# New stage order in the two query stages, the doubled columns copied by ScalarE, and the weight loader moved between the pieces of the lifting

## Chip, cores and metric

One Trainium2 chip, one core. The metric is the device time of one execution in microseconds (us); lower is better. Five engines work in the kernel: TensorE (PE), VectorE (DVE), ScalarE (ACT), GpSimd (POOL) and SyncE (SP, which here only issues DMAs). Each engine takes its instructions in order; between engines they are ordered by semaphores that are written by hand.

## The reference

Two transformer layers run one after the other on x of 8 samples x 512 tokens x 320 features, with a context of 8 x 64 x 192. Layer 0 is plain; layer 1 rounds q, k, v and the softmax weights to 8 bits with one step for the whole tensor.

```python
# layer 0
h1 = _ln(x, n1_g, n1_b)
x = _attn(h1, h1, q1, k1, v1, o1_w, o1_b, heads) + x
h2 = _ln(x, n2_g, n2_b)
x = _attn(h2, context, q2, k2, v2, o2_w, o2_b, heads) + x
h3 = _ln(x, n3_g, n3_b)
...
# layer 1: the same shape, with
q = fq_sym(x @ Wq)            # k, v alike; 20 heads of 16
scores = jnp.einsum('bhnd,bhmd->bhnm', q, k) * dh ** (-0.5)
w = fq_zero(jax.nn.softmax(scores, axis=-1))
out = jnp.einsum('bhnm,bhmd->bhnd', w, v)
```

fq_sym needs the largest magnitude over the whole tensor before any element can be rounded. So in layer 1 the projections are stored first and rounded in a later stage.

## The kernel before

The residual stream x stays in SBUF (x_resid). The program is a row of stages, each a block that every engine enters and leaves together: first loads, context projections, a dense stage with q, k and v (layer 0), self attention, a dense stage with q (the query of the cross attention), cross attention, the feed-forward stage; then the same for layer 1. The change touches three stages: the two dense stages with q ("the query stages", one per layer), and the first block of layer 1's self attention (exact_self_attention).

**A query stage** (dense_phase with main == "q", L497). A sample is 512 tokens in four tiles of 128. Its steps are: oT 0 to 2 (the attention output is turned on PE, in layer 0 only, and split by ACT and DVE into oT_hi and oT_lo; in layer 1 it comes by feature and is only split), oproj 0 to 3 (eight matmuls each, then DVE adds the bank to x_resid, L943), stats (DVE bn_stats, bn_aggr, var_eps, then POOL's power for rstd, L749), norm (DVE writes the normalized rows z, 320 columns and then 64 doubled ones in columns 320 to 383, for each of the four tiles, L959 and L962), zT 0 to 2 (PE turns z, L793; ACT writes h and hT_hi, DVE the difference hT_lo, L969), and q 0 to 2 (eight matmuls each into one of two banks outp; ACT copies the bank to st_hi, L911; then DVE makes st_lo in layer 0, L991, or the maximum in layer 1, L995). The doubled columns exist since the third tile of features has only 64, and the products take its high and low part as two halves of the partitions.

The order of the steps is one list, body, that all engines walk (loop, L624). The table ahead says for which sample a step is done in round i: q for sample i, stats, norm and zT for i + 1, oproj for i + 2 as oT 2, and oT 0 and 1 for i + 3. Every group of banks (oT, oproj, zT, outp) has two banks. On SP a sample's attention output is loaded as soon as that of the one before has been read, and q is stored as it comes out. In layer 0 POOL also splits the weights of the feed-forward stage between the samples (PoolLoader, L226). In layer 1 it adds the next bias to x_resid behind z_ready (L758).

**The first block of layer 1's self attention** (exact_self_attention, L1314). Each sample has a piece of q and of k (128 x 1280) and two of v; POOL loads, scales, rounds and splits them (L1572 to L1598), SP stores the results and loads them back as the stacks q_stack and k_stack, of which there are two. PE makes the 80 score tiles of a sample (L1497), DVE takes the maximum of each (L1531), ACT the exponentials and their sum (L1551). The stack of sample b is loaded when PE is through with sample b - 2. After its last piece POOL loads and splits the weights for what follows (26 jobs of 128 columns: Wq2, Wo1, Wff1) and adds the bias to the eight samples of x_resid (EarlyBias, L290):

```python
                    early.load(pool)
                    for i in range(len(loader.jobs) + 1):
                        loader.turn(pool, i)
                    for b in range(BATCH):
                        early.add(pool, b * TT, TT)
```

The second block of that stage (L1609 on: shifts, transposed scores, exponentials, output products) needs all five engines to have left the first.

## Time and profile before

| | us |
|---|---|
| median of 3 runs (3498.48 to 3504.57) | 3503.2 |
| the profiled execution | 3501.81 |
| its span in the profile | 3500.1 |
| PE busy | 2954.8 (84%) |
| DVE busy | 2168.7 (62%) |
| ACT busy | 1887.1 (54%) |
| POOL busy | 792.6 (23%) |

The page of the profile gives busy time over the whole span. The program is a row of stages with different limits, so the shares alone don't tell what a change in one stage is worth. The trace can be asked for the busy time in a stretch, for the instructions of one engine in order of time (with the idle time ahead of each and who ended it), and for the sum of waits by line. A duration in the timeline can reach a little into the next instruction's, since the engines overlap the end of one with the start of the next. Where instructions follow each other without idle time, the distance of their starts is what each costs.

### The profile page before, as it was taken

Reading aid. Unit: us, or ns where it says so; the run is one execution under the profiler, and the core shown is the slowest. Engines: PE = TensorE matmul, PEld = TensorE weight load, DVE = VectorE, ACT = ScalarE, POOL = GpSimd, SP = SyncE. Lnnn points to the kernel's source line nnn. Section 1 sums busy time; section 2 is a strip of 40 time slices with the busy share of each in tenths; the row PEclk is TensorE's granted clock in tenths of the full one; section 3 lists DMA queues with packets and bytes.
Section 4 is the critical chain, followed back from the end, with each engine's and each line's share of the span. In section 5 each row is a group of like instructions: output and inputs, shape, how many; then the busy total and the mean of one; then the engine's idle time right before and its main releaser. Section 6 shows DMA issues by size and latency. Waiting matters only on the chain. (4 is left out here: it accounts for less than half of the span.)

```text
span 3500.1 us, 47844 instructions
## 1 busy us (share of the span) xinstructions
PE 2954.8 (84%) x15582; PEld 1792.7 (51%) x15594; DVE 2168.7 (62%) x3896; ACT 1887.1 (54%) x3197; POOL 792.6 (23%) x1128
## 2 busy tenths in 40 slices
PE   5979999967697999998959999349987577699999
PEld 3754444456454888886821111011116442588888
DVE  4668888746353443445659999348876586344443
ACT  3427888833253232323559999459983356232322
POOL 0022122113651000000035545820001173200000
PEclk8979999988698999998965555555558899899999
DMA  6653333234662000002586465317532221200000
GB/s 188 209 172 99 104 106 105 83 96 115 147 179 55 10 10 18 9 0 71 151 184 154 105 144 94 62 37 100 83 60 68 74 70 64 57 25 26 16 24 15
DMA packets 369947, 296.61 MB, mean 85 GB/s; under 512 B 186343, under 2 KB 294431, under 8 KB 369759
## 3 DMA queue, kind: packets, MB, share of 16 engines
q1 hardware_dynamic: 361518, 277.73, 32.8%
q0 software_dynamic: 6128, 14.59, 1.7%
q10 hardware_dynamic: 2112, 1.97, 0.3%
q8 instruction: 96, 1.57, 0.2%
q14 instruction: 93, 0.75, 0.1%
HBM read 177.54 MB, written 114.52 MB: 83 GB/s over the span
## 5 line engine op out<-in xcount | busy, mean ns | idle before, releaser
L1297 DVE TENSOR_REDUCE neg_max<-nat 128x1 f32<-128x512 f32 x640 | 400.7, 681 | 66.3 <-PE nat L1160 66.0
L1497 PE MATMUL nat<-k_stack,q_stack 48*128 48x512 bf16 x640 | 380.7, 604 | 70.8 <-DMA k_stack<-k1w 30.2
L1531 DVE TENSOR_REDUCE m_all<-nat 128x1 f32<-128x512 f32 x640 | 423.3, 690 | 17.9 <-PE nat L1497 17.6
L1551 ACT ACTIVATE nat<-nat,m_all 128x512 f32<-128x512 f32 x640 | 427.7, 2128 | 2.9 <-DVE m_all L1531 2.8
L749 POOL TENSOR_TENSOR rstd<-var_eps,neghalf 128x4 f32<-128x4 f32 x48 | 49.0, 1020 | 1592.0 <-DVE var_eps L955 1591.9
L1551 ACT ACTIVATION_READ_ACCUMULATOR nat<-nat,m_all 128x1 f32 x640 | 403.7, 1673 | 0.0
L975 DVE SCALAR_TENSOR_TENSOR ff<-outp,bias,gel 128x512 f32<-128x512 f32 x160 | 120.1, 750 | 419.3 <-PE outp L377 419.3
L1233 ACT ACTIVATE probs<-sT 128x1024 f32<-128x1024 f32 x320 | 328.0, 1027 | 92.4 <-PE sT L1169 84.1
L895 ACT ACTIVATE gel<-outp,bias 128x512 f32<-128x512 f32 x160 | 110.0, 688 | 351.0 <-PE outp L377 351.0
L1730 ACT ACTIVATE exps<-sT 128x1024 f32<-128x1024 f32 x320 | 293.4, 1573 | 7.1 <-PE sT L1679 7.1
L899 ACT CAST ff_hi<-ff 128x512 fp32r<-128x512 f32 x160 | 99.1, 620 | 312.0 <-DVE ff L975 312.0
L1497 PEld LDWEIGHTS nat<-k_stack,q_stack 48*128 48x128 bf16 x640 | 63.8, 101 | 387.3 <-ACT nat L1551 351.1
L1767 DVE TENSOR_SCALAR probs<-exps 128x1024 bf16<-128x1024 f32 x320 | 218.1, 692 | 64.5 <-ACT exps L1730 64.5
L1160 PE MATMUL nat<-k_stack,q_stack 48*128 48x512 f32 x640 | 200.2, 523 | 26.1 <-DMA k_stack<-k_hi 17.3
L1679 PE MATMUL sT<-q_stack,k_stack 51*128 51x512 bf16 x640 | 194.2, 604 | 31.2 <-DMA q_stack<-shift 8.8
L1187 PE MATMUL o_ps<-probs,v_stack 128*32 128x256 f32 x2560 | 199.2, 393 | 1.1 <-issue 1.1
L978 DVE TENSOR_TENSOR ff_lo<-ff,ff_hi 128x512 fp32r<-128x512 f32 x160 | 120.2, 751 | 109.7 <-ACT ff_hi L899 109.7
L969 DVE TENSOR_TENSOR hT_lo<-h,hT_hi 128x512 fp32r<-128x512 f32 x144 | 105.7, 734 | 124.2 <-ACT hT_hi L890 124.1
L1160 PEld LDWEIGHTS nat<-k_stack,q_stack 48*128 48x128 f32 x640 | 79.8, 192 | 169.3 <-DVE neg_max L1297 132.1
L1169 PE MATMUL sT<-q_stack,k_stack 51*128 51x512 f32 x640 | 157.2, 429 | 0.5 <-ACT probs L1233 0.2
L793 PE MATMUL zT<-ident,z 128*128 128x128 f32 x384 | 68.0, 309 | 75.4 <-DVE z L962 64.6
L377 PE MATMUL outp<-hT_hi,Wff_hi 128*128 128x512 f32 x320 | 125.9, 393 | 3.9 <-DVE hT_lo L969 3.9
(495 smaller groups left out, 7180.2 us busy)
## 6 DMA issues: line engine op xcount, KB each, us to landing
v<-vpad SPq DMA_DIRECT2D x64, 320.0 KB, 2.8
q_stack<-q_part SPq DMA_DIRECT2D x90, 160.0 KB, 6.0
k_stack<-k1w SPq DMA_DIRECT2D x90, 160.0 KB, 11.1
q_stack<-q_hi SPq DMA_DIRECT2D x160, 64.0 KB, 2.6
k_stack<-k_hi SPq DMA_DIRECT2D x160, 64.0 KB, 2.2
v_stack<-v SPq DMA_DIRECT2D x40, 256.0 KB, 3.1
q_stack<-q_hi SPq DMA_DIRECT2D x80, 128.0 KB, 2.7
raw<-v SPq DMA_DIRECT2D x16, 640.0 KB, 15.1
```

Of the source, the lines that this page charges most:

```text
L377: mm = pe.matmul(out, stay, move, start=(n == 0), stop=(n == len(terms) - 1))
L1160: pe.matmul(nat[(16 * n + t) % 3][:, :], q_stack[half, n % RING, pr, qt * P:(qt + 1) * P], k_stack[half, n % RING, pr, :], start=True, sto ...
L1169: mm = pe.matmul(sT[use % 2][:, ab, :], k_stack[half, n % RING, pr, kt * P:(kt + 1) * P], q_stack[half, n % RING, pr, :], start=True, stop ...
L1187: mm = pe.matmul(o_ps[VCOL * h:VCOL * h + VCOL, tok], v_stack[:, n % 2, kt, VCOL * h:VCOL * h + VCOL], probs[:, n % 2, h, kt, tok], start= ...
L1233: act.activation(probs[:, n % 2, 2 * pr:2 * pr + 2, kt, :], sT[use % 2][:, :, :], ACT.Exp, scale=DH ** -0.5).then_inc(s["a_turn_free"], 1)
L1297: dve.tensor_reduce(neg_max[:, n % 2, qt, 2 * pr + ab:2 * pr + ab + 1], nat[(16 * (n + 2) + t) % 3][:, :], AX.X, ALU.max, negate=True).the ...
L1497: pe.matmul(bank[i % NAT][:, :], q_stack[half, slot, g, pr, qt * P:(qt + 1) * P], k_stack[half, slot, g, pr, :], start=True, stop=True).th ...
L1531: dve.tensor_reduce(k.m_all[:, column(i // TILES, i % TILES)], bank[i % NAT][:, :], AX.X, ALU.max, negate=True).then_inc(s["e_max_ready"], 1)
L1551: act.activation(b[:, :], b[:, :], ACT.Exp, bias=k.m_all[:, col], accum_out=k.s_all[:, col]).then_inc(s["a_nat_free"], 1)
L1679: mm = pe.matmul(sT[u % TURNS][:, ab, :], k_stack[half, slot, g, pr, kt * P:(kt + 1) * P], q_stack[half, slot, g, pr, :], start=True, stop ...
L1730: act.activation(exps[:, u % EXPS], sT[u % TURNS][:, :, :], ACT.Exp).then_inc(s["a_turn_free"], 1)
L1767: dve.tensor_scalar(probs[:, u % KEPT], exps[:, u % EXPS], ROUND, -ROUND, ALU.add, ALU.add).then_inc(s["e_rounded"], 1)
```

## The change

In the query stages the list body is written in another order: oT 2 and stats come before q 0; q 0, norm, q 1 and q 2 follow; oproj 0 comes behind them; zT 0 and zT 1 follow each other; oproj 2 and 3 come after zT 2. The table ahead stays. In the same stages DVE writes only the 320 columns of z, and one ACT copy of 4 x 64 columns makes the doubled ones; PE waits for the new semaphore z_most ahead of zT 0 and for z_ready ahead of zT 2. POOL's bias add in layer 1 still waits for z_ready. In the first block of layer 1's self attention, four turns of the weight loader and the bias of one sample (beside) come behind every second piece of v, and the load of the bias comes ahead of the pieces.

```diff
--- before.py
+++ after.py
@@ -518,8 +518,8 @@
                 body += [("ff1", c), *between[c]] + ([("ff2", c - 1)] if c else [])
         elif has_o:
             ahead = {"oT": 3, oT[2]: 2, "oproj": 2, "stats": 1, "norm": 1, "zT": 1}
-            body = [items[0], oT[2], ("stats", 0), items[1], ("norm", 0), oproj[0], oproj[1], items[2], zT[0],
-                    oproj[2], zT[1], oproj[3], zT[2], *oT[0:2]]
+            body = [oT[2], ("stats", 0), items[0], ("norm", 0), items[1], items[2], oproj[0], zT[0], zT[1], oproj[1],
+                    zT[2], oproj[2], oproj[3], *oT[0:2]]
         else:
             ahead = {"stats": 1, "norm": 1, "zT": 1}
             body = []
@@ -535,6 +535,7 @@
             if not has_o:
                 turned = {st: x for st, x in turned.items() if st[0] == "zT"}
         groups = {g: n for g, _, n in turned.values()}
+        act_doubles = has_o and main == "q"
         n_items = len(items)
         n_v = sum(x == "v" for x, _ in items)
         n_qk = n_items - n_v
@@ -810,7 +811,9 @@
                         product(pe, bank_of(st, r)[:, 0:D], wo, slice(0, D), oT_hi, oT_lo,
                                 slice(m * P, (m + 1) * P), True).then_inc(s[turned[st][0] + "_full"], 1)
                     elif kind == "zT":
-                        if m == 0:
+                        if m == 0 and act_doubles:
+                            pe.wait_ge(s["z_most"], at["z_most"] + b + 1)
+                        if m == (2 if act_doubles else 0):
                             pe.wait_ge(s["z_ready"], at["z_ready"] + b + 1)
                         turn_tile(st, b, r, z)
                     elif kind == "ff1":
@@ -877,6 +880,9 @@
                             wait_past(act, s[g + "_full"], at[g + "_full"] + (b - 1) * uses + turned[oproj[TT - 1]][1] + 1)
                         src = attn[:, m, :] if by_feature else bank_of(st, r)[:, :]
                         act.copy(oT_hi[:, m, :], src).then_inc(s["oT_hi_done"], 1)
+                    elif kind == "norm" and act_doubles:
+                        act.wait_ge(s["z_most"], at["z_most"] + b + 1)
+                        act.copy(z[:, :, D:ZCOL], z[:, :, 2 * P:D]).then_inc(s["z_ready"], 1)
                     elif kind == "zT":
                         bank_full(act, st, b)
 
@@ -956,12 +962,13 @@
                     elif kind == "norm":
                         dve.wait_ge(s["rstd_ready"], at["rstd_ready"] + b + 1)
                         for t in range(TT):
-                            dve.tensor_scalar(z[:, t, 0:D], xt(b, t), mv[:, t, 0:1], rstd[:, t:t + 1],
-                                              ALU.subtract, ALU.mult)
-
-                            ins = dve.tensor_scalar(z[:, t, D:ZCOL], xt(b, t)[:, 2 * P:D], mv[:, t, 0:1],
-                                                    rstd[:, t:t + 1], ALU.subtract, ALU.mult)
-                        ins.then_inc(s["z_ready"], 1)
+                            ins = dve.tensor_scalar(z[:, t, 0:D], xt(b, t), mv[:, t, 0:1], rstd[:, t:t + 1],
+                                                    ALU.subtract, ALU.mult)
+
+                            if not act_doubles:
+                                ins = dve.tensor_scalar(z[:, t, D:ZCOL], xt(b, t)[:, 2 * P:D], mv[:, t, 0:1],
+                                                        rstd[:, t:t + 1], ALU.subtract, ALU.mult)
+                        ins.then_inc(s["z_most" if act_doubles else "z_ready"], 1)
                         if load and isinstance(b, int) and b == 0:
                             split_weights()
                     elif kind == "zT":
@@ -1399,6 +1406,7 @@
             round_col = sb("round_col", [P, 1], own=own)
             loader = PoolLoader(nc, s, own, next_weights, 128)
             early = EarlyBias(nc, s, own, k, bias)
+            PER_BATCH = -(-len(loader.jobs) // BATCH)
             first_scaled = [t.rearrange("p x w -> p (x w)").bitcast(F32) for t in (v_whole[:, :, :], q_parts[:, 1, 0:2, :])]
             ones_b = q_parts[0:3, 1, 2, 0:TOK]
             bank = [psum(f"nat{i}", [P, TOK], own) for i in range(NAT)]
@@ -1560,8 +1568,14 @@
                         ins.then_inc(s["a_part_chain"], 1)
                         wait(pool, "a_part_chain", count[0])
 
+                    def beside(b):
+                        for i in range(PER_BATCH * b, PER_BATCH * (b + 1)):
+                            loader.turn(pool, i)
+                        early.add(pool, b * TT, TT)
+
                     chained(pool.memset(ones[:, :], 1.0))
                     pool.memset(ones_b, 1.0).then_inc(s["e_ones"], 1)
+                    early.load(pool)
                     wait(pool, "e_inv_step", 1)
                     wait(pool, "scalar_chain", 2)
                     for i in range(FIRST, len(pieces)):
@@ -1598,11 +1612,10 @@
                             pool.tensor_scalar(v_whole[:, r, :], lifted[:, :], -ROUND, None, ALU.add
                                                ).then_inc(s["e_v_whole"], 1)
                             wait(pool, "e_v_whole", b + 1)
-                    early.load(pool)
-                    for i in range(len(loader.jobs) + 1):
+                            if b % 2:
+                                beside(b // 2)
+                    for i in range(PER_BATCH * BATCH, len(loader.jobs) + 1):
                         loader.turn(pool, i)
-                    for b in range(BATCH):
-                        early.add(pool, b * TT, TT)
             loader.passed()
             early.passed()
```

In the query stage of layer 0 these are DVE's steps at the start of a round before; two more pairs of z, the adds of oproj 0 and 1 and the third st_lo follow. Names are tiles; oT_lo and hT_lo are the low parts of the turned attention output and of the normalized features, oproj the banks of the output projection.

```order
L991 TENSOR_TENSOR st_lo<-outp_222,st_hi 128x512
L939 TENSOR_TENSOR oT_lo<-oT_216,oT_hi 128x512
L950 BN_STATS bn<-x_resid 128x6 x4
L953 BN_AGGR mv<-bn 128x2 x4
L955 TENSOR_SCALAR var_eps<-mv 128x4
L991 TENSOR_TENSOR st_lo<-outp_223,st_hi 128x512
L959 TENSOR_SCALAR z<-x_resid,mv,rstd 128x320
L962 TENSOR_SCALAR z<-x_resid,mv,rstd 128x64
L959 TENSOR_SCALAR z<-x_resid,mv,rstd 128x320
L962 TENSOR_SCALAR z<-x_resid,mv,rstd 128x64
```

And these are the same steps now, from oT 2 on.

```order
L945 TENSOR_TENSOR oT_lo<-oT_217,oT_hi 128x512
L956 BN_STATS bn<-x_resid 128x6 x4
L959 BN_AGGR mv<-bn 128x2 x4
L961 TENSOR_SCALAR var_eps<-mv 128x4
L998 TENSOR_TENSOR st_lo<-outp_223,st_hi 128x512
L965 TENSOR_SCALAR z<-x_resid,mv,rstd 128x320 x4
L998 TENSOR_TENSOR st_lo<-outp_224,st_hi 128x512
L998 TENSOR_TENSOR st_lo<-outp_223,st_hi 64x512
L949 TENSOR_TENSOR x_resid<-x_resid,oproj_219 128x320
L976 TENSOR_TENSOR hT_lo<-h_209,hT_hi 128x512 x2
```

The low part st_lo of q 0 moved from ahead of the statistics to behind them, norm has four instructions where it had eight, and the other two st_lo now stand between norm and the first hT_lo.

On ACT, in the query stage of layer 1, one round now reads as follows (attn_T is the attention output by feature, outp the banks of q, zT those of the turned rows).

```order
L882 CAST oT_hi<-attn_T 128x512
L917 COPY st_hi<-outp_407 128x512
L885 COPY z<-z 128x4x64
L917 COPY st_hi<-outp_408 128x512
L917 COPY st_hi<-outp_407 64x512
L894 ACTIVATE h_394<-zT_406,b_col,g_col 128x512
L896 ACTIVATE hT_hi<-zT_406,b_col,g_col 128x512
```

The copy of z stands ahead of the copies of q 1 and q 2, and both stand ahead of the reads of zT 0; before, no instruction of ACT waited for norm there.

On POOL, in the first block of layer 1's self attention, this now stands behind the second piece of v of a sample (stage is the loader's buffer, Wff the feed-forward weights).

```order
L1612 TENSOR_SCALAR v_whole<-lifted 128x1280
L1586 TENSOR_SCALAR lifted<-raw,inv_step 128x1280
L1612 TENSOR_SCALAR v_whole<-lifted 128x1280
L246 DMA stage<-in_L_xattn_Wff 128x2x128
L251 DMA stage<-in_L_xattn_Wff 64x128 x2
L261 CAST tail_hi<-stage 128x128
L262 CAST Wff_hi<-stage 128x2x128
L266 TENSOR_TENSOR Wff_tail<-stage,tail_hi 128x128
L270 CAST Wff_tail<-stage 64x128
L271 TENSOR_TENSOR Wff_lo<-stage,Wff_hi 128x2x128
```

Before, the next piece (lifted) came right behind v_whole, and all turns of the loader behind the last piece.

## Rows read from the trace of the kernel before

**Rows 1.** Busy time by stretch: the two query stages, then attention's first block.

```profile
core 0: us, PE busy (x) PEld busy (x) DVE busy (x) ACT busy (x) POOL busy (x), PEclk, DMA share, GB/s
756.50:893.60 137.10, 99.14 (x508) 82.42 (x508) 93.11 (x204) 50.52 (x80) 53.88 (x68) 0.88 0.44 121
2652.10:2775.80 123.70, 92.09 (x444) 72.46 (x444) 84.28 (x203) 51.03 (x80) 27.70 (x14) 0.89 0.23 69
1795.00:2222.00 427.00, 379.99 (x638) 63.49 (x634) 422.68 (x640) 424.15 (x1274) 227.73 (x207) 0.50 0.61 124
...
2227.00:2295.00 68.00, 0.00 (x0) 0.00 (x0) 0.00 (x0) 0.00 (x0) 56.34 (x80) 0.50 0.31 46
```

**Rows 2.** Timeline of POOL behind its last piece: start, duration, engine, line, operation.

```profile
2145.97 0.73 POOL L246 DMA_DIRECT2D stage<-in_L_xattn_Wq  x1
...
2272.63 22.70 POOL L306 TENSOR_TENSOR x_resid<-x_resid,early_bias 128x1280 f32<-128x1280 f32 x8
```

**Rows 3.** Waits of POOL, 2100 to 2300: total us, times, longest.

```profile
POOL tail_hi L261 <- DMA stage<-in_L_xattn_Wff: 16.0, 3, 7.9
```

**Rows 4.** Timeline of SP: its last loads in the block, its first in the next.

```profile
2226.01 1.39 SPq L1376 DMA_DIRECT2D k_stack<-k1w  x3
2302.11 0.39 SPq L1638 DMA_DIRECT2D v_stack<-v1w  x1
```

**Rows 5.** Timeline of POOL: first piece of samples 2 and 3, first of the last two [idle before].

```profile
1835.84 1.33 POOL L1572 TENSOR_SCALAR lifted<-raw,inv_step 128x1280 f32<-128x1280 f32 x1 [17.44 <-DMA raw<-q]
...
1872.88 1.33 POOL L1572 TENSOR_SCALAR lifted<-raw,inv_step 128x1280 f32<-128x1280 f32 x1 [11.37 <-DMA raw<-q]
...
2135.20 1.33 POOL L1572 TENSOR_SCALAR lifted<-raw,inv_step 128x1280 f32<-128x1280 f32 x1 [27.98 <-DMA raw<-v]
```

**Rows 6.** Timeline of SP: k of the last sample stored, its stack loaded.

```profile
2097.34 0.32 SPq L1437 DMA_DIRECT2D k1w<-k_whole  x1
2114.98 2.70 SPq L1376 DMA_DIRECT2D q_stack<-q_part  x6
```

**Rows 7.** Timeline of DVE, one round of layer 1's query stage.

```profile
2688.21 0.69 DVE L969 TENSOR_TENSOR hT_lo<-h,hT_hi 128x512 fp32r<-128x512 f32 x1 [0.83 <-ACT hT_hi L890]
2688.82 1.29 DVE L939 TENSOR_TENSOR oT_lo<-attn_T,oT_hi 128x512 fp32r<-128x512 f32 x2
...
2693.83 1.67 DVE L950 BATCH_NORM_STATS2 bn<-x_resid 128x6 f32 x4
...
2696.06 0.17 DVE L955 TENSOR_SCALAR var_eps<-mv 128x4 f32<-128x4 f32 x1
...
2697.36 0.45 DVE L959 TENSOR_SCALAR z<-x_resid,mv,rstd 128x320 f32 x1 [0.40 <-POOL rstd L749]
2697.72 0.31 DVE L962 TENSOR_SCALAR z<-x_resid,mv,rstd 128x64 f32 x1
...
2699.68 0.88 DVE L943 TENSOR_TENSOR x_resid<-x_resid,oproj 128x320 f32 x2
...
2705.78 0.69 DVE L969 TENSOR_TENSOR hT_lo<-h,hT_hi 128x512 fp32r<-128x512 f32 x1 [0.83 <-ACT hT_hi L890]
```

**Rows 8.** Timeline of ACT in the same stage: one copy of a bank of q.

```profile
2694.59 0.59 ACT L911 COPY st_hi<-outp 128x512 f32<-128x512 f32 x1 [1.58 <-PE outp L377]
```

**Rows 9.** Timeline of DVE, one round of layer 0's query stage.

```profile
795.32 0.69 DVE L969 TENSOR_TENSOR hT_lo<-h,hT_hi 128x512 fp32r<-128x512 f32 x1 [0.74 <-ACT hT_hi L890]
...
803.85 0.45 DVE L959 TENSOR_SCALAR z<-x_resid,mv,rstd 128x320 f32 x1 [0.46 <-POOL rstd L749]
...
807.92 0.87 DVE L943 TENSOR_TENSOR x_resid<-x_resid,oproj 128x320 f32 x2
...
815.11 0.69 DVE L969 TENSOR_TENSOR hT_lo<-h,hT_hi 128x512 fp32r<-128x512 f32 x1 [1.31 <-ACT hT_hi L890]
```

**Rows 10.** Timeline of PE in that round: q 0, oT 2, the wait for z.

```profile
796.15 0.49 PE L377 MATMUL outp<-hT_hi,q_hi 128*128 128x512 f32 x1 [1.47 <-DVE hT_lo L969]
798.09 0.60 PE L793 MATMUL oT<-ident,attn_nat 128*128 128x128 f32 x4
808.15 0.65 PE L793 MATMUL zT<-ident,z 128*128 128x128 f32 x4 [3.26 <-DVE z L962]
```

More of the change, by code:

```diff
@@ L582, in dense_phase @@
             "d_const", "attn_in_loaded", "oT_split", "oT_hi_done", "bias2_added", "bn_done",
-            "aggr_done", "stats_ready", "rstd_ready", "z_ready", "hT_hi_done",
+            "aggr_done", "stats_ready", "rstd_ready", "z_most", "z_ready", "hT_hi_done",
             "g_full", "a_full", "gelu_done", "ff_used", "ff_hi_done", "ff_split", "ffT_used", "y_drained",
@@ L1019, in dense_phase @@
                 "bn_done": TT * BATCH, "aggr_done": TT * BATCH, "stats_ready": BATCH, "rstd_ready": BATCH,
-                "z_ready": BATCH, "hT_hi_done": 3 * BATCH,
+                "z_most": BATCH * act_doubles, "z_ready": BATCH, "hT_hi_done": 3 * BATCH,
                 "g_full": FFC * BATCH * ff, "a_full": FFC * BATCH * ff, "gelu_done": FFC * BATCH * ff,
```

## The prediction

> **What bounds the kernel.** The page's shares come first: PE 84%, POOL 23%. Neither tells what the change is worth, since it touches three stages with different limits. So I cut the span at the stages [rows 1]. In attention's first block of layer 1, DVE (422.7) and ACT (424.2) are busy for all of 427 us, with 640 tiles, 0.667 us each, 53.4 a sample: this pace is set by neither PE nor POOL. Then come 68 us in which PE, DVE and ACT do nothing and POOL alone works. In the two query stages no engine is full: PE 99 of 137 us and 92 of 124, DVE 93 and 84. There a chain sets the time, not an engine. The two stretches are cut at the third hT_lo of a sample (I call its end T), from sample 0 to 7: 19.6 us a round in layer 0, 17.7 in layer 1. The timelines of the single rounds show the chain [rows 7, 9, 10].
>
> **Part 1, POOL's tail.** Behind its last piece POOL runs 26 loader turns from 2145.97 to 2272.63, then 22.7 us of bias to 2295.33 [rows 2]. Without the 16.0 us in which it waited for transfers [rows 3] a turn costs (126.7 - 16.0) / 26 = 4.26 us, and the bias 2.84 a sample. SP, the last of the others, is through at 2226.01 + 1.39 = 2227.4, and the next block starts at 2302.1, 6.8 behind POOL [rows 4]. The change puts four turns and one bias, 4 x 4.26 + 2.84 = 19.9 us, behind each sample's second v. POOL's own pieces take 1872.88 - 11.37 - 1835.84 = 25.7 us a sample [rows 5]. Together 45.6, below the 53.4 of the tiles. POOL's idle gaps are 17.4 and 11.4 for the first two and reach 28 later [rows 5], so POOL falls 2.5 + 8.5 = 11 us behind at the third and gets this back. Nobody sees it: SP stores the last k at 2097.3 and can load its stack only at 2115.0, when PE has left the old one [rows 6], and PE needs it a further 53 us on. What is queued behind the loader's waits is the next sample's lifting alone. The last bias then ends near 2150, long before ACT and DVE.
>
> The next block starts 6.8 behind SP instead, at 2234.2: **-67.9 us**. Bounds: if entering took no time at all it were -75, which I don't believe; -71 if half of the 6.8 belongs to POOL's tail. On the other side, SP's last stack load is now in flight when the next block wants its first data; the longest wait for a transfer in such a stretch is 7.9 [rows 3], which leaves -60. The earlier bias load lies in a stretch where POOL waits for data, at nothing.
>
> The rule that speaks against this move: POOL's loader starts its DMAs itself. The trace has some 16 of the turns (up to 2222) beside DVE's reduces and the rest alone, and DVE kept 0.667 us a tile all through [rows 1]. The Trainium skill, page "SBUF — State Buffer", section "SBUF: two separate sides", says that a DMA issued by GpSimd can't get its descriptors written while VectorE runs a two-port operation, 620 ns becoming 3100; by it, 12 DMAs would add 30 us to each sample and this part would end near +7. The same page exempts reduces on this chip, and the 4.26 of the trace is on that side.
>
> **Part 2, layer 1's query stage.** Before: q 0, its copy and maximum stand ahead of the statistics, so z ends at 2699.7, 10.8 us behind T = 2688.9; from there to the next T (2706.5) are 6.8 [rows 7]. Now behind T stand on DVE two adds (0.9), three oT_lo (two take 1.29, so 0.6 each: 1.8), the statistics (2693.83 to 2696.06: 2.2), the wait for POOL's rstd (1.3 from var_eps to z) and four z at 0.36: 7.7. The four small z that go cost 0.22 each, 0.8 in all, and the rest of the 3.1 is the order. PE needs three q (1.94 each [rows 10], less the first's start: 5.7) and oproj 0 (1.2, an estimate by its columns, 320 of 512): 6.9, so it still waits 0.8 for z.
>
> The price is on ACT. It now waits for z_most with the copies of q 1 and q 2 queued behind it. After z it makes the doubled columns, 256 of them, where 512 take 0.59 [rows 8]: between 0.3 and 0.6, I take 0.45. Then two copies of 0.6, to T + 9.3, while zT 0 is full near T + 8.5. So the path from z grows from 6.8 to 7.6, and a round is 15.3. POOL's bias add starts 0.45 later behind z_ready; it stretches hT_lo as before. In the last round, without oproj and oT, PE's three q bind: 5.7 + 6.8 = 12.5. Stage: 6 x 15.3 + 12.5 = 104.3 for 123.7: **-19.4**. Ends: without ACT's queue -25; with z's path 1.5 longer and PE at half clock for some of the q, -10.
>
> **Part 3, layer 0's query stage.** One round was 795.3 to 815.1, 19.8 [rows 9]. Here PE also turns oT; oT 2 now stands ahead of q 0 and, with two banks, waits until DVE is through with oT 0: T + 1.9. So q 0 starts at T + 2.4 (before: T + 0.15) and q 1 ends at T + 6.3. q 2 needs the bank of q 0, whose st_lo now stands behind the statistics, about T + 6.6; q 2 ends at T + 8.6 and oproj 0 at T + 9.8. DVE: z starts at T + 7.1; eight z took 4.07 beside POOL's loader (803.85 to 807.92), half of that is 2.0: T + 9.1. So PE, not z, decides, at T + 9.8, where z before came at T + 11.9 and PE had waited 3.3 for it [rows 10]. From zT 0 to T took 7.9 with oproj 2 and 3 between the turns; now only oproj 1 stands there. Layer 1's path less its stretched hT_lo gives 6.0; I take 6.3. Round 16.1, and 16.5 since the clock was granted at 0.88 [rows 1], so that parts ran at 1.2 GHz. Last round 12.5. Stage: 6 x 16.5 + 12.5 = 111.5 for 137.1: **-25.6**. Ends: -32 at full clock, -12 if the path from z stays at 7.9 and oT 2's wait costs 0.6 more.
>
> Sum: -67.9 - 19.4 - 25.6 = -113, from the profiled 3501.8: **3389 us**. The median of the runs is 3503.2, 1.4 above, within their spread.
>
> **Rivals.**
> 1. *The query stages give nothing.* The new waits (oT 2 on two banks, ACT behind z_most, q 2 behind st_lo) use up what the order frees; a T-to-T time of 19.6 and 17.7 again. For it: three new waits in a chain. Against it: by the rows each ends before z did. Time: 3501.8 - 67.9 = 3434. At half the gain, 3411.
> 2. *The loader's transfers hold POOL, and PE waits for stacks.* If every turn waits 7.9, the longest of rows 3, POOL's round is 45.6 + 31.6 = 77.2 against 53.4. Six rounds bring 143 us; 58 of that are slack (from the last k stored at 2097 to its use at 1795 + 7 x 53.4 = 2169, less some 13 for store and load). So +85: 3474. It ends **slower than before** from a wait of 9.1 us a turn on; at 12 it is 6 x (45.6 + 48 - 53.4) - 58 = +183: 3572. For it: 16 us of waits in three turns. Against: the other turns hardly waited, and the three fell into stack loads, which beside doesn't meet. The skill's rule of part 1 would act in just this way.
> 3. *The query stages gain more*: fewer idle gaps keep PE at 2.4 GHz and ACT's copies find a gap: -32 and -25, with -71 for the tail: 3374.
>
> **How the numbers follow.** Forecast 0.75 (3376 to 3408), rival 1 0.13 (its half case at 3411 is the likelier), rival 3 0.07, rival 2 0.05, of which 0.02 end slower than before. The predicted time is the forecast's. The range goes from 3372 (all bounds good) to 3422 (tail -60, query stages -10 and -12, which is also beyond the half case of rival 1); it leaves out the full rival 1 and rival 2, less than 2 in 10. A measurement of this kernel tells about 0.2% (7 us) from no change. Faster 0.97, same 0.01, slower 0.02.
>
> **What would show it.** Right: between the blocks of attention no stretch with POOL alone; the first block still 427 us; the gaps ahead of lifted q near 8 us from sample 4 on; T to T near 15.3 and 16.5; ACT's copy near 0.45; PE's wait for z below 1 us. Wrong: idle time of DVE on PE's scores in the first block (rival 2); T to T at 17 or more, with the wait at oT 2 or at ACT's first read of zT 0 (rival 1); a longer start of the second block.

## The result, and the profile after

The changed kernel takes **3393.3 us** (4 runs, 3391.8 to 3395.2) against 3502.3 of the kernel before in the same comparison: ratio 0.969, 95% interval 0.967 to 0.971. A later comparison gave 0.970 (0.969 to 0.972). The forecast was 3389, range 3372 to 3422.

The profiled execution has a span of 3390.7 us for 3500.1, which is 109.4 less. Cut at the places of the prediction (T: end of the third hT_lo of a sample):

| stretch | before | after | difference | forecast |
|---|---|---|---|---|
| start to T of sample 0, layer 0's query stage | 756.5 | 755.3 | -1.3 | 0 |
| layer 0's query stage, T 0 to T 7 | 137.1 | 119.7 | **-17.4** | -25.6 |
| T 7 to the first block of attention | 874.4 | 874.7 | +0.3 | 0 |
| first block's start to the second's | 534.2 | 459.2 | **-75.0** | -67.9 |
| second block to T 0 of layer 1's query stage | 349.9 | 349.9 | 0.0 | 0 |
| layer 1's query stage | 123.7 | 106.7 | **-17.0** | -19.4 |
| T 7 to the end | 724.3 | 725.2 | +0.9 | 0 |

Busy time by stretch in the changed kernel: layer 0's query stage, attention's first block, what lies between that block and the next, layer 1's query stage. The columns are those of [rows 1].

```profile
755.30:874.90 119.60, 90.95 (x520) 74.68 (x518) 88.26 (x177) 52.76 (x88) 52.97 (x68) 0.96 0.50 139
1776.00:2203.00 427.00, 379.98 (x638) 63.52 (x634) 422.80 (x640) 424.24 (x1274) 288.93 (x297) 0.50 0.60 129
2203.00:2209.00 6.00, 0.00 (x0) 0.00 (x0) 0.59 (x2) 4.59 (x15) 0.00 (x0) 0.50 1.01 124
2558.80:2665.50 106.70, 84.88 (x445) 70.07 (x444) 79.96 (x177) 52.53 (x88) 27.54 (x14) 0.94 0.26 80
```

Of the 68 us in which POOL worked alone 6 are left, and they belong to SP's loads and ACT's end. In the first block DVE and ACT do what they did, in the same time, with 61 us more of POOL beside them. In the query stages PE is idle for less time (28.7 and 21.8 us, where it was 38.0 and 31.6), and the clock was granted at 0.96 and 0.94 for 0.88 and 0.89.

The end of the first block, on DVE (the 624 reduces without a gap, then the second block's first instruction) and SP (last stack loads):

```profile
1789.47 413.95 DVE L1539 TENSOR_REDUCE m_all<-nat 128x1 f32<-128x512 f32 x624 [3.89 <-PE nat L1505]
2208.84 0.82 DVE L1754 TENSOR_REDUCE red<-s_all 128x1 f32<-128x640 f32 x1 [5.41 <-PEq L1422]
```

```profile
2202.73 2.69 SPq L1383 DMA_DIRECT2D q_stack<-q_part  x6
2205.46 2.82 SPq L1383 DMA_DIRECT2D k_stack<-k1w  x6
2208.79 0.39 SPq L1651 DMA_DIRECT2D v_stack<-v1w  x1
```

SP is through at 2205.46 + 2.82 = 2208.28, and the next block begins 0.5 us behind it, where it began 6.8 behind POOL [rows 4]. That is 6.3 of the 7.1 us by which this term was better than forecast; the other 0.8 are that SP itself is through 458.7 us behind the start of the first block for 459.5. The second block's first probs comes 21.1 us behind its start for 19.3, but the stretch from there to the next query stage is no longer for it (349.9 both times).

POOL in the same block: the bias of samples 4, 5, 6 and 7, one piece's first step, and its waits from 1760 to 2230.

```profile
2035.02 2.87 POOL L306 TENSOR_TENSOR x_resid<-x_resid,early_bias 128x1280 f32<-128x1280 f32 x1
...
2076.44 0.29 POOL L261 CAST tail_hi<-stage 128x128 fp32r<-128x128 f32 x1 [6.51 <-DMA stage<-in_L_xattn_Wff]
...
2087.14 2.87 POOL L306 TENSOR_TENSOR x_resid<-x_resid,early_bias 128x1280 f32<-128x1280 f32 x1
2090.01 1.32 POOL L1586 TENSOR_SCALAR lifted<-raw,inv_step 128x1280 f32<-128x1280 f32 x1
...
2133.97 2.87 POOL L306 TENSOR_TENSOR x_resid<-x_resid,early_bias 128x1280 f32<-128x1280 f32 x1
...
2146.74 2.88 POOL L306 TENSOR_TENSOR x_resid<-x_resid,early_bias 128x1280 f32<-128x1280 f32 x1
```

```profile
POOL tail_hi L261 <- DMA stage<-in_L_xattn_Wff: 33.4, 5, 7.6
POOL lifted L1586 <- DMA raw<-v: 13.3, 1, 13.3
POOL tail_hi L261 <- DMA stage<-in_L_xattn_Wq: 12.4, 1, 12.4
POOL tail_hi L261 <- DMA stage<-in_L_xattn_Wo: 7.9, 1, 7.9
POOL lifted L1586 <- DMA raw<-q: 7.1, 1, 7.1
```

The last bias ends at 2149.6. That looks like the forecast's "near 2150", but the forecast counted on the time line of the kernel before, in which the first block starts at 1767.9; now it starts at 1749.6. So the last bias ends 400 us behind the block's start where 382 was forecast, 18 us later. And the gaps of 8 us ahead of lifted q, which the forecast wanted to see, are not there: the lifting at 2090.01 begins right behind the bias, and the two waits of lifted for raw in the list lie at the start of the block. Instead POOL waits once in each sample that has turns, 6 to 12 us, for one transfer of the loader: 53.7 us in seven waits. It is the transfer that it starts first, 2.5 us or less behind SP's stack loads of the same sample (1854.78 behind 1850.12 + 2.82 in the second). From bias to bias it takes 52.1 (2087.14 - 2035.02), just below the 53.1 of DVE's 80 tiles (413.95 / 624 x 80). It is behind from the first sample on and stays there.

One round of layer 1's query stage on DVE, the third of the seven, with the two waits of PE for transpositions. It starts at T = 2588.46:

```profile
2590.15 0.49 DVE L949 TENSOR_TENSOR x_resid<-x_resid,oproj 128x320 f32 x1 [1.29 <-PE oproj L377]
2592.49 1.66 DVE L956 BATCH_NORM_STATS2 bn<-x_resid 128x6 f32 x4
2594.30 0.38 DVE L959 BATCH_NORM_AGGREGATE mv<-bn 128x2 f32<-128x6 f32 x4
2594.72 0.17 DVE L961 TENSOR_SCALAR var_eps<-mv 128x4 f32<-128x4 f32 x1
2594.95 0.69 DVE L1002 TENSOR_REDUCE amax<-st_hi 128x512 f32 x1
2596.02 1.52 DVE L965 TENSOR_SCALAR z<-x_resid,mv,rstd 128x320 f32 x4 [0.39 <-POOL rstd L750]
```

```profile
2597.68 1.09 PE L794 MATMUL zT<-ident,z 128*128 128x128 f32 x8 [0.89 <-DVE z L965]
2601.79 0.66 PE L794 MATMUL zT<-ident,z 128*128 128x128 f32 x4 [1.86 <-DVE hT_lo L976]
```

PE's wait for z is 0.9 us where it was 1.2 (the row shows the forecast's "below 1"). The third zT now waits 1.9 us for hT_lo, with nothing but projections behind it: that wait is new in size and matters below. Of the first six rounds four take 14.8 to 14.9 us and two, this one among them, 16.2 and 16.3, for a mean of 17.7 before. In the short ones z ends at T + 7.7; in the long ones an add to x_resid waits about 1.3 us for its projection, and z ends at T + 9.1 and 9.2. From the start of zT 0 to the next T both take 7.0.

One round of layer 0's query stage (T = 789.57), on DVE, and two of the loader's steps beside it on POOL:

```profile
797.08 2.05 DVE L965 TENSOR_SCALAR z<-x_resid,mv,rstd 128x320 f32 x4 [0.41 <-POOL rstd L750]
...
801.99 2.23 DVE L976 TENSOR_TENSOR hT_lo<-h,hT_hi 128x512 fp32r<-128x512 f32 x2 [0.22 <-ACT hT_hi L896]
804.14 0.47 DVE L949 TENSOR_TENSOR x_resid<-x_resid,oproj 128x320 f32 x1
805.85 0.69 DVE L976 TENSOR_TENSOR hT_lo<-h,hT_hi 128x512 fp32r<-128x512 f32 x1 [1.23 <-ACT hT_hi L896]
```

```profile
797.80 1.09 POOL L251 DMA_DIRECT2D stage<-in_L_xattn_ff_w  x2
801.53 1.54 POOL L271 TENSOR_TENSOR w_lo<-stage,w_hi 128x640 fp32r<-128x640 f32 x1
```

Two such subtractions that follow each other take 1.3 us when POOL is quiet (two oT_lo of the same size, 1.29); here they take 2.2: the first begins while POOL's subtraction runs, and ends only 0.55 us behind it, at 1.63. The four z take 2.05 for 1.52 in layer 1. The one that is stretched most (797.94, 0.84 us for 0.45) runs while POOL starts its transfers, from 797.02 to 798.89.

### The profile page after: what moved, and what is told of

Its sections match the earlier page's. It is cut to its first block and busy times, and to the rows that moved or that the text cites. A ratio compares the mean times of both kernels' runs of the same rounds, so it can differ in the third digit from the quotient of the medians.

```text
span 3390.7 us, 47793 instructions
## 1 busy us (share of the span) xinstructions
PE 2941.4 (87%) x15594; PEld 1783.3 (53%) x15594; DVE 2157.9 (64%) x3832; ACT 1890.0 (56%) x3213; POOL 792.2 (23%) x1128
## 5 line engine op out<-in xcount | busy, mean ns | idle before, releaser
L1505 PE MATMUL nat<-k_stack,q_stack 48*128 48x512 bf16 x640 | 380.7, 605 | 70.1 <-DMA k_stack<-k1w 29.4
L1505 PEld LDWEIGHTS nat<-k_stack,q_stack 48*128 48x128 bf16 x640 | 63.9, 101 | 386.5 <-ACT nat L1559 351.0
L1167 PE MATMUL nat<-k_stack,q_stack 48*128 48x512 f32 x640 | 199.7, 521 | 26.0 <-DMA k_stack<-k_hi 17.4
L976 DVE TENSOR_TENSOR hT_lo<-h,hT_hi 128x512 fp32r<-128x512 f32 x144 | 114.6, 802 | 106.8 <-ACT hT_hi L896 106.1
L1692 PEld LDWEIGHTS sT<-q_stack,k_stack 51*128 51x128 bf16 x640 | 33.9, 101 | 182.4 <-ACT exps L1743 166.4
```

The lines of the kernel that those rows point to most:

```text
L1167: pe.matmul(nat[(16 * n + t) % 3][:, :], q_stack[half, n % RING, pr, qt * P:(qt + 1) * P], k_stack[half, n % RING, pr, :], start=True, sto ...
L1505: pe.matmul(bank[i % NAT][:, :], q_stack[half, slot, g, pr, qt * P:(qt + 1) * P], k_stack[half, slot, g, pr, :], start=True, stop=True).th ...
L1692: mm = pe.matmul(sT[u % TURNS][:, ab, :], k_stack[half, slot, g, pr, kt * P:(kt + 1) * P], q_stack[half, slot, g, pr, :], start=True, stop ...
```

## The experiments

**One part of the change at a time.** Three kernels: POOL's part alone (the old body, DVE makes all of z), the order alone, and the copy on ACT alone. Each is made from the changed kernel by taking parts of its diff back. The first takes back these two, the second only the lower one, the third the upper one; the second and third also have POOL's tail of the kernel before.

```diff
-            body = [oT[2], ("stats", 0), items[0], ("norm", 0), items[1], items[2], oproj[0], zT[0], zT[1], oproj[1],
-                    zT[2], oproj[2], oproj[3], *oT[0:2]]
+            body = [items[0], oT[2], ("stats", 0), items[1], ("norm", 0), oproj[0], oproj[1], items[2], zT[0],
+                    oproj[2], zT[1], oproj[3], zT[2], *oT[0:2]]
...
-        act_doubles = has_o and main == "q"
+        act_doubles = False
```

> Only POOL's move: the loader's turns and the bias come between the pieces, the query stages are as before. Theory (the tail was 68 to 75 us in which POOL worked alone, and nothing else of the change touches it): the stretch from the first block's start to the second block's start is 75 us shorter, 3501.8 becomes 3427 to 3430, and the query stages keep 19.6 and 17.7 us a round. Rival (the moved work slows DVE or ACT by sharing SBUF with them): the 624 last reduces of the first block take more than the 414 us of before. Rival (the entry of the second block is dear in itself): 6.8 us again behind the last engine.

> Only the new order of the steps; DVE still makes the doubled columns, POOL's tail stands. Theory (the order frees the most of it; the doubled columns cost DVE 0.8 us in layer 1 and 2 in layer 0 on the path to z, but ACT's queue behind z_most costs 0.6 of that back): -25 to -32 us for both stages, so 3470 to 3477, rounds near 15.0 in layer 1 and 18 in layer 0. Rival (the order alone gives nothing since z stays the bound): 3495 to 3502.

> Only ACT's copy of the doubled columns, in the old order; POOL's tail stands. Theory: z comes 0.8 us earlier in layer 1 and about 2 in layer 0, and zT 0 waits only for z_most, so up to 7 x (0.8 + 2) = 20 us; part of it is kept, since PE waited for z there in each round: -10 to -20, 3482 to 3492. Rival (ACT's queue eats it): 3498 to 3504.

And the opposite of the first, order and copy with POOL's tail kept:

```diff
-                            if b % 2:
-                                beside(b // 2)
-                    for i in range(PER_BATCH * BATCH, len(loader.jobs) + 1):
+                    for i in range(len(loader.jobs) + 1):
                         loader.turn(pool, i)
+                    for b in range(BATCH):
+                        early.add(pool, b * TT, TT)
```

> The order and the copy of the doubled columns on ACT, with POOL's turns and bias additions in the tail behind the last piece as in the kernel before. If the terms simply add: 3502.3 minus 17.4 minus 17.0, about 3467 us; the stretch from the first block's start to the second's is again 534 us, with the entry gap of 6.8 us. If the query stages' gain needs POOL's part of the change: the rounds of layer 0 and 1 are not 17.1 and 14.8 as in the changed kernel but nearer 18 and 15.5 of the order alone.

| kernel | us | ratio to before | layer 0 stage | layer 1 stage |
|---|---|---|---|---|
| before | 3498 to 3502 | 1 | 137.1 | 123.7 |
| POOL's part alone | 3425.7 | 0.980 (0.978 to 0.982) | 133.0 | 122.9 |
| order alone | 3468.3 | 0.992 (0.990 to 0.994) | 122.8 | 107.8 |
| copy on ACT alone | 3479.2 | 0.996 (0.994 to 0.997) | 121.7 | 122.4 |
| order and copy, POOL's tail kept | 3462.5 (one run) | | 119.3 | 106.7 |
| the change | 3393.3 | 0.969 (0.967 to 0.971) | 119.7 | 106.7 |

POOL's part and the query stages' parts add up: the stages have the same length with and without it. The rivals of the first expectation are out: the 624 reduces take 413.94 us, and the second block begins 0.5 us behind SP.

Within layer 1's stage the order and the copy add up too: the order gives 15.9 of the 17.0, the copy alone 1.3. In layer 0 they don't. The order alone gives 14.3 and the copy alone 15.4, but both together 17.4. (The old order's stage took 137.1 in one profile and 133.0 in the other, POOL's part alone, so each of the three can be some 4 us smaller; the sum of the first two stays well above the third.) The rounds show why. Before, zT 0 starts at T + 12.1, and from there to the next T are 7.6 us. The order alone leaves its start at T + 12.0, where PE still waits 1.4 us for z, and gains on the path behind it, 5.9. The copy alone starts it at T + 10.0, as four z take half of what eight took (4.1 us beside the loader), and leaves the path at 7.3. With both it starts at T + 10.2, without a wait for z, but the path is 6.8 and not 5.9: as z is ready earlier, the first hT_lo (801.99) falls into the loader's subtraction (801.53 to 803.07), while with the order alone that has ended (805.14) ahead of the first hT_lo (805.55, 0.69 us).

The order alone came out just below its expected 3470 to 3477, the copy alone just below its 3482 to 3492.

**How long entering a block takes, and who sets it.** With PER_BATCH = 1, 19 of the loader's turns stand behind the last piece again, but the bias is added inside:

```diff
-            PER_BATCH = -(-len(loader.jobs) // BATCH)
+            PER_BATCH = 1
```

> One loader turn per sample inside the first attention block instead of four; the other 18 or so follow the last piece. POOL rounds get shorter and the last pieces come earlier, but some 90 us of turns stand behind them: POOL would end near 2217 us (last piece near 2128, 19 turns of 4.7 us) against the 2208.8 at which the second block starts in the changed kernel. Theory A (POOL's end releases the second block, and the 6.8 us from SP's last load to the next block's first instruction in the kernel before was POOL's leaving): the second block starts near 2223, 6 to 7 us after POOL's last instruction, and the kernel takes about 3407 us. Theory B (the 6.8 us belongs to SP or to every block start): it starts within 1 us behind whatever ended last, near 2217, 3401 us. If POOL's tail costs nothing at all: 3393 us.

It took 3415.8 us (one run). POOL's last instruction, and the second block's first on DVE:

```profile
2226.81 0.72 POOL L271 TENSOR_TENSOR Wff_lo<-stage,Wff_hi 128x256 fp32r<-128x256 f32 x1
```

```profile
2234.35 0.82 DVE L1754 TENSOR_REDUCE red<-s_all 128x1 f32<-128x640 f32 x1 [30.24 <-PEq L1422]
```

2234.35 - 2227.53 = 6.8 us, as before, though the 19 turns took 94 us where I had 89. In the kernel with order and copy alone it is 6.8 as well (bias to 2275.22, DVE at 2282.04). Where POOL is through early the block begins 0.5 us behind SP's last load (in the changed kernel and in POOL's part alone, 2227.30 to 2227.82). Theory A holds: the 6.8 go with POOL's end. What POOL does in them no row shows. Nor is it shown that it is SP that releases the block in the other kernels: ACT's last instruction there ends 1.4 us ahead of the block, and no run moved the one without the other.

**How far POOL may fall behind.** Behind each sample's bias come 12 chained memsets (EXTRA is 12; the edit also raises the count of the semaphore that chains them):

```diff
                         early.add(pool, b * TT, TT)
+                        for _ in range(EXTRA):
+                            chained(pool.memset(scaled[:, 1, :], 0.0))
```

> The changed kernel with 12 chained memsets of 128x1280 on POOL behind each sample's turns and bias in the first attention block (into a buffer that is rewritten before it is read, so the output is the same), about 1.25 us each, 15 us per sample, 120 us in all. Of these the 6.7 us per sample that POOL waits for the loader's transfers can hide a part. Theory A (POOL runs behind DVE in the whole block, and the 58 us that I worked out are what it may fall behind before DVE waits): POOL's rounds grow by 8 to 15 us, together 66 to 120, so DVE's reduces of this block end 8 to 60 us later and the kernel takes 3401 to 3453 us. Theory B (POOL's pieces are no condition of this block at all): DVE's reduces stay at 414 us, and at most the start of the second block is later. Theory C (there is no slack any more, POOL paces the block already): the whole 66 to 120 us show, 3459 us or more.

It took 3452.9 us (one run). DVE in the block:

```profile
1786.12 146.60 DVE L1542 TENSOR_REDUCE m_all<-nat 128x1 f32<-128x512 f32 x224 [2.75 <-PE nat L1508]
1942.60 50.35 DVE L1542 TENSOR_REDUCE m_all<-nat 128x1 f32<-128x512 f32 x80 [9.88 <-PE nat L1508]
2010.22 50.35 DVE L1542 TENSOR_REDUCE m_all<-nat 128x1 f32<-128x512 f32 x80 [17.28 <-PE nat L1508]
2077.78 50.35 DVE L1542 TENSOR_REDUCE m_all<-nat 128x1 f32<-128x512 f32 x80 [17.20 <-PE nat L1508]
...
2213.85 50.35 DVE L1542 TENSOR_REDUCE m_all<-nat 128x1 f32<-128x512 f32 x80 [18.70 <-PE nat L1508]
```

and its cause, in the waits of PE (the total of the block; 29.4 us of it, in two waits, are at the block's start in the changed kernel too):

```profile
PE nat L1508 <- DMA k_stack<-k1w: 109.6, 7, 24.5
```

POOL's round grew from 52 to 67 us, and from the fourth sample on DVE keeps POOL's pace. Theory A in kind, but not with its 58 us: the stack load that DVE first waited for was issued at 1926.3, in the changed kernel at 1903.4 with a block that began 3.4 us later. So it was 26.3 us later, and DVE waited 9.9 of them. The slack of the changed kernel at that sample is about 16 us. The time is at the upper end of what theory A gave, 6 us below theory C: counted from the block's start, the last sample's stack load is issued 91 us later than in the changed kernel, and the second block begins 66 us later.

**Is POOL's loader what keeps layer 0's rounds at 17?** The turns of the loader in the query stages all behind the last sample's statistics:

```diff
                         step(("stats", 0), b, b % 2)
-                        for i in range(b * per_sample, (b + 1) * per_sample):
-                            loader.turn(pool, i)
-                    loader.turn(pool, BATCH * per_sample)
+                    for i in range(BATCH * per_sample + 1):
+                        loader.turn(pool, i)
```

> In the query stages the weight loader's turns all come after the statistics steps of all samples instead of three or so behind each sample's. The whole kernel may be longer, as these turns then stand behind the stage; what counts is the time from the third hT_lo of one sample to that of the next in the two query stages. Theory A (the loader's arithmetic on POOL slows DVE's and POOL's own steps: hT_lo of 1.1 us taking 2.0, statistics late): layer 0 rounds fall from 17.1 to about 15.5 and those of layer 1, 14.8 to 16.3, to about 14.5; the last layer 0 round is 12.5 to 14 instead of 15.8. Theory B (POOL beside has no part in it; the chain aggregate, variance, root, z, transposition has this length by itself): 17.1 and 14.8 stay within 0.3.

The kernel as a whole is longer, 3417.3 us, since these turns now end behind the stage. The stage itself took 110.3 us for 119.7, its rounds 16.2 for 17.0 and the last 13.2 for 15.8. Layer 1 is as it was (107.6). DVE in a round of layer 0:

```profile
798.75 1.52 DVE L964 TENSOR_SCALAR z<-x_resid,mv,rstd 128x320 f32 x4 [0.38 <-POOL rstd L750]
...
803.69 0.69 DVE L975 TENSOR_TENSOR hT_lo<-h,hT_hi 128x512 fp32r<-128x512 f32 x1 [0.79 <-ACT hT_hi L895]
805.02 0.69 DVE L975 TENSOR_TENSOR hT_lo<-h,hT_hi 128x512 fp32r<-128x512 f32 x1 [0.65 <-ACT hT_hi L895]
```

z is back at 1.52, and no hT_lo is stretched until the last round, where the turns begin. Theory A for layer 0 (somewhat less than it said, 16.2 for 15.5), theory B for layer 1: the alternation of 14.8 and 16.3 there has another cause. The gain of a round in layer 0 is all on the path from zT 0 to the next T, 5.8 us for 6.8. zT 0 itself starts at T + 10.4 for 10.2, right behind PE's oproj 0, so the shorter z is worth nothing there.

**Three other orders.** Each is one step moved in the body of the changed kernel, which ran once more with them.

> The changed kernel once more, for comparison with the orders beside it: 3393 us, rounds of 17.1 and of 14.8 to 16.3.

```diff
-            body = [oT[2], ("stats", 0), items[0], ("norm", 0), items[1], items[2], oproj[0], zT[0], zT[1], oproj[1],
+            body = [oT[2], ("stats", 0), items[0], items[1], ("norm", 0), items[2], oproj[0], zT[0], zT[1], oproj[1],
```

> In the body of the query stages the normalization stands behind the second query item instead of the first. ACT's copy of the doubled columns then has st_hi of q1 ahead of it, not behind. If ACT's queue around the copy matters (it waits about 4.5 us for z with q1's high part behind it): q1's high part is done earlier, q2 starts earlier, rounds fall by 0.3 to 0.7, the two stages by 4 to 10 us together. If z is what is late anyway (its end comes from root and aggregate on POOL), nothing moves by more than 0.2 per round: 3393 within 3. If DVE's st_lo of q1 now stands ahead of z and z comes later for it: rounds longer by up to 0.8, 3393 to 3405.

```diff
-            body = [oT[2], ("stats", 0), items[0], ("norm", 0), items[1], items[2], oproj[0], zT[0], zT[1], oproj[1],
+            body = [oT[2], ("stats", 0), items[0], ("norm", 0), items[1], items[2], oproj[0], zT[0], oproj[1], zT[1],
```

> In the body the second output projection stands between the first and the second transposition of z instead of behind the second. If the rounds of 16.3 among those of 14.8 in layer 1 come from a late projection (DVE waited 1.3 us for it there): they fall to about 15, some 4 us over the stage; but the second transposition, and with it hT_lo, then come later by the 1.0 to 1.6 us of a projection in each round: if that decides, rounds are longer by about 1 us, 14 us over both stages, 3407.

```diff
             body = [oT[2], ("stats", 0), items[0], ("norm", 0), items[1], items[2], oproj[0], zT[0], zT[1], oproj[1],
-                    zT[2], oproj[2], oproj[3], *oT[0:2]]
+                    oproj[2], zT[2], oproj[3], *oT[0:2]]
```

> In the body the third output projection stands ahead of the third transposition. The third transposition waits 1.7 to 1.9 us for hT_lo on PE with the projection queued behind it. If that wait holds the projection back and the projection is what DVE's x_resid lacks in the 16.3 rounds: PE fills the wait, rounds fall by 0.5 to 1.3 in layer 1 and up to 0.5 in layer 0, together 5 to 12 us, 3381 to 3388. If the third transposition starts later for it, since the projection is longer than the wait or banks are not yet free: same or up to 5 us slower.

| kernel | us | ratio to before | layer 0 stage | layer 1 stage |
|---|---|---|---|---|
| the change again | 3396.0 | 0.970 (0.969 to 0.972) | 117.9 | 106.6 |
| norm behind q 1 | 3395.7 | 0.970 (0.968 to 0.972) | 119.6 | 107.5 |
| second projection ahead of zT 1 | 3393.5 | 0.970 (0.968 to 0.971) | 117.8 | 106.4 |
| third projection ahead of zT 2 | **3379.1** | 0.965 (0.963 to 0.966) | 113.6 | 98.8 |

Neither of the first two moves anything beyond the spread of the changed kernel itself: ACT's queue around the copy is not in the chain, and nor is the place of the second projection. The third is faster than both kernels. PE's waits in layer 1's stage there:

```profile
PE outp L377 <- DVE hT_lo L976: 5.3, 7, 2.3
PE oproj L377 <- DVE x_resid L949: 4.5, 12, 0.4
PE zT L794 <- DVE hT_lo L976: 3.0, 1, 3.0
PE zT L794 <- DVE z L965: 1.4, 6, 0.2
```

In the changed kernel zT waited 14.3 us in seven times for hT_lo; only one such wait is left. The projection fills it, and x_resid is not late any more: DVE waited 4.0 us in three times for a projection there, and now not once. Every round is 14.3 us, the last 13.1, without the alternation.

The second and the third of these together, projections and transpositions in turn:

```diff
-            body = [oT[2], ("stats", 0), items[0], ("norm", 0), items[1], items[2], oproj[0], zT[0], zT[1], oproj[1],
-                    zT[2], oproj[2], oproj[3], *oT[0:2]]
+            body = [oT[2], ("stats", 0), items[0], ("norm", 0), items[1], items[2], oproj[0], zT[0], oproj[1], zT[1],
+                    oproj[2], zT[2], oproj[3], *oT[0:2]]
```

> Projections and transpositions in turn: first projection, first transposition, second projection, second transposition, third projection, third transposition, fourth projection. If only the wait of the third transposition for hT_lo was worth filling (14.0 and 14.3 us of PE waits over the two stages in the changed kernel, 6.3 and 3.0 with the third projection ahead of it): as with that order alone, 3379 within 3. If the second projection's two microseconds more ahead of the second transposition delay the first hT_lo: rounds longer by up to 1 us, up to 3393. If it also evens out DVE's x_resid adds: rounds shorter by up to 0.3, 3375.

3380.5 us (5 runs), ratio 0.966 (0.964 to 0.968): no better than the third alone, as the first of the expectations said. In its profile the query stages take 109.8 and 98.8, 3.8 less in layer 0 than with the third alone, but layer 0's cross attention, which the edit doesn't touch, takes 211.6 us for 205.4 (from its first maximum to the first gel of the feed-forward stage), with POOL's parts waiting 7.1 us for PE there, for 1.5. Why is open; it wasn't tried.

## Why the prediction was right, point by point

**Sign and size.** 3389 against 3393, with all three terms of the right sign. The errors of the three have opposite signs, 7.1 us better, 8.2 and 2.4 worse; that only 3.5 are left of them is luck. The range's ends are those of the bounds taken from the median of the runs: -132 and -82 give 3371 and 3421, 1 us below what it says.

**POOL's tail, -67.9 against -75.0.** The step "the next block starts 6.8 behind SP instead" failed. The 6.8 belong to POOL's end, as the run with one turn showed, and the bound of -75, "which I don't believe", is what came. Nothing of the lower bound (-60) was seen but the 1.8 us by which the second block's first probs is later, and they don't reach the end of the stretch.

**POOL's round, 45.6 against 52.1.** "Nobody sees it" held, but not by the working. The term of 4.26 us a turn left out the 16.0 us of waits for transfers. Beside the block such a wait comes in each sample with turns, 6 to 12 us, and POOL never gets its 11 us back. The step of rival 2 that failed with it is "the three fell into stack loads, which beside doesn't meet": beside the pieces, the turns begin just behind the stack loads of every sample. The slack was mis-sized too: the 58 us were read at the last sample of the kernel before, where POOL had run ahead; at the fourth sample of the changed kernel they are 16. Both errors were hidden because 52.1 is 1.0 us below 53.1. Nothing in the working gave that margin, so "nobody sees it" was right by luck.

This makes rival 2 dearer than I wrote. At a wait of 7.9 in every turn it would cost, as an estimate, 6 x (77.2 - 53.4) - 16 = 127 us, which is slower than before (3516, not 3474). Its ground held: one turn in four does wait 6 to 12 us. Its chance of 0.05 was too small for a margin of 1 us a round.

**The rule on DMAs started by POOL.** Its DMA issues take 0.74 to 0.79 us, and 1.04 to 1.07 for two, beside DVE's reduces in the changed block; in the tail before, where DVE was idle, they took 0.74 and 1.04. In the kernel before, a 128 KB transfer of the loader landed 2.6 us behind its issue (median) both beside the reduces (2141 to 2222) and in the idle tail (2241 to 2275). The 427 us of the block are unchanged. So the reduces don't hold back the loader's transfers, which is the exemption that the Trainium skill's page "SBUF — State Buffer" makes for reduces, and not its rule.

**Layer 1's query stage, -19.4 against -17.0.** The copy of the doubled columns took 0.41 (0.45 forecast), and in the 14.8 us rounds z ended at T + 7.7, where forecast. But the path behind z is 7.0 to 7.1 and not 7.6: the step "the path from z grows from 6.8 to 7.6" was mis-sized. And the forecast had no round of 16.3, in which x_resid waits for a projection and z ends 1.4 later. That the mean of six, 15.3, is the forecast is these two errors cancelling. The error of the term is in the last round, 14.9 for 12.5. "PE's three q bind" did not hold: z ended at T + 7.4, PE waited 0.3 for it, and the path was 7.4 where the sum took 6.8, the path of before. In the changed kernel run again, with x_resid in time, the last round was 13.5 (z at T + 6.0).

**Layer 0's query stage, -25.6 against -17.4.** The failed step is "layer 1's path less its stretched hT_lo gives 6.0; I take 6.3". In layer 0 hT_lo is stretched as well, by POOL's loader, and the path measures 6.8; with the loader away it is 5.8. The four z are stretched too, but that was in the sum: "half of that is 2.0" took them with the loader beside. In the last round, where DVE's subtractions meet the loader twice (2 hT_lo in 3.25 us, the third in 2.03), it took 15.8 for 12.5. That is 3.3 of the 8.2; the six other rounds bring 4.8, of which 1.5 are one round of 18.5 in which x_resid waited for a projection (it is 17.0 in the changed kernel run again). With the loader away the stage took 110.3 where I had 111.5. So the 6.0 of the working is about the path of a stage without POOL's loader, and the 6.3 made of it is 0.5 short of the one with it. (The 7.9 that it calls "from zT 0 to T" is counted from the end of z; from zT 0 it was 7.65.) Up to zT 0 the forecast was 0.4 short: q 0 began at T + 2.45 (2.4), PE's wait at oT 2 was 1.0, z ended at T + 9.6 (9.1), q 2 began at T + 7.2 (6.6) behind st_lo, and zT 0 at T + 10.2 (9.8).

The Trainium skill, page "SBUF — State Buffer", section "SBUF: two separate sides", has the rule behind it: GpSimd and those operations of VectorE that read two tensors in SBUF (against a GpSimd instruction that reads SBUF), or run in a two-port mode, take a shared pair of ports for a whole instruction, and the other waits. The trace agrees: hT_lo is stretched beside POOL's subtraction (2.23 for 1.3), z while POOL starts its transfers (2.05 for 1.52), neither of them in the same rounds with the loader away, and the reduces of the attention block not at all (422.8 us for the 640 of them, 422.7 before, with 61 us more of POOL beside).

**Rivals 1 and 3.** With -34.4 of -45.0 from the query stages rival 1 is out; of its new waits the ones at oT 2 (1.0 us) and of q 2 for st_lo (0.8 us) are there, and both were in the sum. Rival 3 was right on the tail and wrong on the stages.

## What to carry to other kernels

Where one engine's tail stands alone ahead of a block boundary, moving it into a block that another engine bounds can be worth all of it and the time from that engine's end to the next block: here 75.0 us. Its new round must be counted with the transfer waits it will meet there, and its slack read at the earliest consumer, not the last. Two edits of one chain need not add: in layer 0 what the one brings forward meets another engine's work, in layer 1 they add. So ask what is late next, and give the waiting engine a step whose inputs are ready: here one projection ahead of a waiting transposition was worth a further 14 to 17 us (3379.1 against 3393.3 and 3396.0).

## What the runs showed of the hardware

- The second block of layer 1's self attention begins 6.8 to 7.0 us behind POOL's last instruction where POOL is last (in six of the kernels), and 0.5 us behind SP's last load where POOL is through early.
- The first transfer that POOL starts behind SP's stack loads is waited for 6 to 12 us, the others of the same size not at all.
- 80 reduces take 50.35 us (0.629 each) behind a stall and 53.1 (0.663) in the steady stream. In the steady stream PE's weight loads wait 351.0 us, in 617 times, for ACT to leave a bank, so that DVE alone doesn't set the pace of that block.
- A subtraction of DVE with both inputs in SBUF that began during one of POOL's (1.54 us) took 1.63 us for 0.69; with the loader away it took 0.69.
